# Four-layer cross-attention model: channel chunks summed on the vector engine ahead of the norms' matmuls, and half of a feed-forward projection moved across a loop boundary

## What is computed

```python
x = L0(x, ctx)   # grouped-query cross-attention, + x, then layer norm
x = L1(x, ctx)   # recurrent layer
x = L2(x, ctx)   # norm -> multi-head cross-attention, + x; norm -> 512-2048-512 MLP, + residual
x = L3(x, ctx)   # recurrent layer, same form as L1

# norm, everywhere, over the 512 channels of a token
m = x.mean(-1);  v = ((x - m) ** 2).mean(-1);  y = (x - m) / sqrt(v + eps) * w + b

# recurrent layer
xa = ln(x);  five token-shifted mixes of xa give r, k, v, w, g
s_t = k_t v_t^T + w_t * s_(t-1);  out_t = r_t (u k_t v_t^T + s_(t-1))      # 16x16 state per head
x1 = x + (head_norm(out) * g) @ Wo.T
xc = ln(x1);  sx2 = shift(xc) - xc
xk2 = xc + sx2 * ffn_maa_k;  xr2 = xc + sx2 * ffn_maa_r
return x1 + sigmoid(xr2 @ Wfr.T) * (square(relu(xk2 @ Wfk.T)) @ Wfv.T)
```

## Time and profile before

| | us |
|---|---|
| median of 3 runs | 3214.15 |
| lowest, highest | 3211.52, 3218.05 |
| the profiled execution, its own time | 3217.8 |
| its span in the trace | 3216.0 |
| PE busy | 2880.1 (90%) |
| DVE busy | 1985.7 (62%) |
| ACT busy | 1361.0 (42%) |
| POOL busy | 664.9 (21%) |

### The profile page before, as it was taken

How to read it: one execution, slowest core, us unless ns; L and a number is a source line. 1 busy time by engine, 2 the same in 40 slices (tenths; PEclk the granted TensorE clock), 3 DMA queues, 4 the chain that set the end, 5 groups by cost and what they waited for, 6 DMA issues and landing times.

```text
span 3216.0 us, 54227 instructions
## 1 busy us (share of the span) xinstructions
PE 2880.1 (90%) x18304; PEld 2244.7 (70%) x18304; DVE 1985.7 (62%) x4824; ACT 1361.0 (42%) x3457; POOL 664.9 (21%) x436
## 2 busy tenths in 40 slices
PE   6999998878999999689999998899987889999986
PEld 6555555866888887586545544799987768888866
DVE  2778777348899999523555555210100689999993
ACT  0888887522343333253444444321321233333332
POOL 0011010024444444200000000000000444444440
PEclk9999999978999999799999999899998889999998
DMA  2100100323333333200000000300002333332340
GB/s 102 35 25 31 33 31 3 124 63 93 83 88 88 87 83 93 79 26 19 20 19 27 18 28 1 144 1 0 0 0 85 85 94 86 88 88 83 87 115 19
DMA packets 96305, 182.76 MB, mean 57 GB/s; under 512 B 10138, under 2 KB 87514, under 8 KB 92862
## 3 DMA queue, kind: packets, MB, share of 16 engines
q1 hardware_dynamic: 96190, 181.27, 18.3%
HBM read 171.34 MB, written 9.90 MB: 56 GB/s over the span
## 4 chain that ended last, share of the span: by engine, by line
PE 64%; DVE 13%; issue 11%; ACT 8%; DMA 1%; POOL 1%; DVEq 0%; SPq 0%; ACTq 0%; POOLq 0%
PE psum L466 18%; PE psum L271 11%; PE psum L1812 5%; PE psum L1694 4%; PE psum L1259 3%; DVE psum L665 3%; PE psum L457 2%; ACT arena L1460 2%; ACT arena L2002 2%; PE psum L1749 2%; PE psum L1707 2%; PE psum L473 2%; PE psum L1271 2%; DVE arena L688 2%; PE psum L247 2%
## 5 line engine op out<-in xcount | busy, mean ns | idle before, releaser
L466 PE MATMUL psum<-arena 128*128 128x200 f32 x4096 | 785.9, 351 | 87.1 <-DVE arena L844 34.4
L466 PEld LDWEIGHTS psum<-arena 128*128 128x128 f32 x4096 | 733.6, 200 | 175.5 <-issue 110.2
L1063 POOL TENSOR_TENSOR arena<-arena 128x800 f32<-128x800 f32 x256 | 455.5, 1779 | 513.5 <-DVE psum L665 513.4
L680 DVE TENSOR_TENSOR_SCAN arena<-arena,psum 128x808 f32<-128x808 f32 x256 | 469.9, 1836 | 59.9 <-PE psum L457 47.2
L271 PE MATMUL psum<-arena 128*128 128x200 f32 (+1 forms) x2048 | 354.0, 335 | 21.7 <-DMA arena<-L_w 20.3
L271 PEld LDWEIGHTS psum<-arena 128*128 128x128 f32 x2048 | 351.2, 192 | 23.4 <-DMA arena<-L_w 20.3
L1460 ACT ACTIVATE arena<-arena 100x361 f32<-100x361 f32 x512 | 300.5, 590 | 76.9 <-DVE arena L1371 75.3
L1045 POOL TENSOR_TENSOR arena<-arena 128x800 f32<-128x800 f32 x80 | 140.4, 1755 | 856.0 <-DVE arena L688 695.9
L1371 DVE CUSTOM_DVE_ANT_0 arena<-psum,arena 100x361 f32<-100x361 f32 x512 | 254.0, 529 | 45.5 <-ACT arena L1460 37.9
L665 DVE TENSOR_TENSOR psum<-arena 128x808 f32<-128x808 f32 x256 | 262.5, 1025 | 4.6 <-DVE arena L680 0.5
L1259 PEld LDWEIGHTS psum<-arena 100*128 100x128 f32 x1536 | 145.9, 141 | 131.1 <-ACT arena L1472 60.3
(11 more groups left out here) (129 smaller groups left out, 4069.1 us busy)
## 6 DMA issues: line engine op xcount, KB each, us to landing
arena<-v_rows SPq DMA_DIRECT2D x512, 202.0 KB, 3.2
arena<-ctxT SPq DMA_DIRECT2D x32, 722.0 KB, 4.3
arena<-L_w SPq DMA_DIRECT2D x8, 1152.0 KB, 15.2
arena<-L_w SPq DMA_DIRECT2D x8, 1024.0 KB, 9.8
v_rows<-arena SPq DMA_DIRECT2D x32, 202.0 KB, 2.1
arena<-L_fc SPq DMA_DIRECT2D x4, 1024.0 KB, 7.8
arena<-L_pj SPq DMA_DIRECT2D x4, 1024.0 KB, 15.6
arena<-xT SPq DMA_DIRECT2D x4, 800.0 KB, 9.9
```

What stands on the lines that cost most here:

```text
L466: mm = pe.matmul(chunk(bank, j), m.W[n][:, k, c * P:(c + 1) * P], src[:, k, :], start=k == 0, stop=k == C - 1)
L680: dve.tensor_tensor_scan(m.ring[n % 4].rearrange("p j e -> p (j e)"), m.we[:, cc].rearrange("p j e -> p (j e)"), m.kv, 0.0, ALU.mult, ALU. ...
L1063: pool.tensor_tensor(sv, sv, rb, ALU.mult).then_inc(sem("r_states"), 1)
```

## The change

It has two parts.

**Attention layers' norms.** A class FoldedNorm replaces Norm in L0 and L2 (not in L1 and L3). DVE adds the four channel chunks of a group into one 128x200 tile (tensor_reduce over a view whose innermost axis is the chunk, so consecutive elements read lie 800 bytes apart), and PE then needs one matmul per mean; the squares are treated alike for the variance. The two logarithms of a pair are taken one after the other and then the two exponentials, where before each group had logarithm and exponential together. On PE one group's projection of the next pair now stands between the means and the variances, and the other behind the variances. In L2 ahead of the attention the order becomes: means of t+1, query projection of (t, 0), variances of t+1, query projection of (t, 1).

**Recurrent layers.** fr half 0 moves from the end of a period behind the mean at the start of the next, its tanh moves with it, DVE makes xr2 ahead of step 14 where it stood behind it, and POOL's multiplication of step 13 waits for product 15 where it waited for product 14.

```diff
+class FoldedNorm(Norm):
+    def dve_fold(self, dve, src, i):
+        dve.tensor_reduce(self.fold, src.rearrange("p c n -> p n c"), mybir.AxisListType.X,
+                          ALU.add).then_inc(self.folds.sem, 1)
+    def pe_mean(self, pe, i):
+        pe.wait_ge(self.folds.sem, self.folds.at(i, self.nth))
+        pe.matmul(self.mean_ps, self.core.mean_w, self.fold, start=True, stop=True).then_inc(self.mu.sem, 1)
...
+        pe.matmul(self.var_ps, self.core.mean_w, self.fold, start=True, stop=True).then_inc(self.var.sem, 1)
```

```diff
 # recurrent layers, PE, start of a period
                 m.n1.pe_mean(pe, lambda c: X[:, c, ds(g + 1, N)], f)
+            if tail:
+                wait(pe, "ffn_mix", t, 8)
+                if rec:
+                    wait(pe, "mix_term", i, 20)
...
+                project_half("fr", m.xr2, 0, 4, "ffn_r_sum")
             if back:
                 reduce(6, b)
 # ACT
             if tail:
-                wait(act, "ffn_r_sum", t, 2)
-                act.activation(half(m.thr, 1), full(5), ACT.Tanh, scale=0.5).then_inc(sem("ffn_tanh"), 1)
+                wait(act, "group_done", t)
+                for h in range(2):
+                    wait(act, "ffn_r_sum", t, h + 1)
+                    act.activation(half(m.thr, h), full(4 + h), ACT.Tanh, scale=0.5).then_inc(sem("ffn_tanh"), 1)
 # POOL
                 if rec:
+                    if n == 13:
+                        wait(pool, "kv", i, 16)
                     pool.tensor_tensor(sv, sv, rb, ALU.mult).then_inc(sem("r_states"), 1)
```

```diff
 # L0 behind its attention, PE
             for u in range(2):
-                pe.wait_ge(residual_added.sem, residual_added.at(t, 4 * u + 4))
-                norms[u].pe_mean(pe, lambda c: X[:, c, bass.ds(t * (2 * N) + u * N, N)], t)
+                norms[u].pe_mean(pe, t)
+            if more:
+                pe.wait_ge(residual_added.sem, residual_added.at(t, 4))
+                project(pe, core, 2, Wo, ...)
             for u in range(2):
                 norms[u].pe_var(pe, t)
...
 # DVE
             for u in range(2):
                 dve.wait_ge(residual_added.sem, residual_added.at(t, 4 * u + 4))
+                norms[u].dve_fold(dve, xo(t, u), t)
+            for u in range(2):
                 dve.wait_ge(norm_ready.sem, norm_ready.at(t))
                 norms[u].dve_center(dve, xo(t, u), t)
+            for u in range(2):
+                norms[u].dve_fold_squares(dve, t)
             for u in range(2):
                 norms[u].scale(dve, t)
 # ACT
             for u in range(2):
-                norms[u].act_rstd(act, t)
+                norms[u].act_log(act, t)
+            for u in range(2):
+                norms[u].act_exp(act, t)
```

The order in L2 ahead of the attention, on PE:

```diff
-        statistics(0)
-        statistics(1)
-        queries(0, True)
+        statistics(0)
+        variances(0)
+        for u in range(2):
+            if u == 0:
+                statistics(1)
+            queries(0, u, True)
+            if u == 0:
+                variances(1)
         with pe.Fori(1, pairs - 1) as t:
             statistics(t + 1)
-            queries(t, False)
-        queries(pairs - 1, False)
+            queries(t, 0, False)
+            variances(t + 1)
+            queries(t, 1, False)
+        for u in range(2):
+            queries(pairs - 1, u, False)
```

More of the change, by code:

```diff
@@ L487, in body @@
                 m.n1.pe_mean(pe, lambda c: X[:, c, ds(g + 1, N)], f)
+            if tail:
+                wait(pe, "ffn_mix", t, 8)
+                if rec:
+                    wait(pe, "mix_term", i, 20)
+                elif back:
+                    wait(pe, "bonus", b, 1)
+                project_half("fr", m.xr2, 0, 4, "ffn_r_sum")
             if back:
@@ L839, in body @@
                 mix_term(4)
-            step(14)
             if back:
@@ L845, in body @@
                                              m.xs2[:, c, :, 1:E], ALU.mult, ALU.add).then_inc(sem("ffn_mix"), 1)
+            step(14)
             step(15)
@@ L1031, in body @@
                     act.activation(half(m.kk, h), half(m.ff, h), ACT.Square).then_inc(sem("ffn_squared"), 1)
-                wait(act, "ffn_r_sum", b, 1)
-                wait(act, "group_done", b)
-                act.activation(half(m.thr, 0), full(4), ACT.Tanh, scale=0.5).then_inc(sem("ffn_tanh"), 1)
         turns(act, body)
@@ L1105, in gqa_attention @@
     told = norm_signals(core, name)
-    norms = [Norm(core, told, u, 1, 2 * u, 2 * u + 1).memory(r) for u in range(2)]
+    folds = s("folds", 4)
+    norms = [FoldedNorm(core, told, u, 1, 2 * u, 2 * u + 1).memory(r).signals(folds) for u in range(2)]
     s2 = [n.s2.rearrange("p c n -> p (c n)") for n in norms]
@@ L1563, in mha_attention @@
     told = norm_signals(core, name)
-    norms = [Norm(core, told, u, 0, 2 * u, 2 * u + 1).memory(r) for u in range(2)]
+    folds = s("folds", 4)
+    norms = [FoldedNorm(core, told, u, 0, 2 * u, 2 * u + 1).memory(r).signals(folds) for u in range(2)]
     over = r.at
@@ L1829, in vector @@
         for p in pr:
-            dve.memset(p[:, S:3 * P], 0.0).then_inc(zeroed.sem, 1)
+            dve.memset(p[:, S:3 * P], 0.0)
         def norm_ahead(t):
+            for u in range(2):
+                dve.wait_ge(norms[u].var.sem, norms[u].var.at(t))
+                norms[u].dve_fold(dve, X[:, :, bass.ds(t * (2 * N) + u * N, N)], t)
             for u in range(2):
@@ L1934, in behind_it @@
                 dve.wait_ge(residual_added.sem, residual_added.at(t, 4 * u + 4))
+                norms[u].dve_fold(dve, xo(t, u), t + behind)
+            for u in range(2):
                 dve.wait_ge(fc_sum.sem, fc_sum.at(t))
                 norms[u].dve_center(dve, xo(t, u), t + behind)
+            for u in range(2):
+                norms[u].dve_fold_squares(dve, t + behind)
             for u in range(2):
@@ L2018, in scalar @@
             for u in range(2):
-                norms[u].act_rstd(act, t + behind)
+                norms[u].act_log(act, t + behind)
+            for u in range(2):
+                norms[u].act_exp(act, t + behind)
             for u in range(2):
```

90 lines of the change are left out of this document (55 added, 35 removed).

## The result

The changed kernel takes 3175.6 us (median of 4, 3173.7 to 3181.3), the kernel before beside it 3215.2. The ratio is 0.9878, 95% interval 0.9864 to 0.9891: 39.6 us, or 1.2%, less. The forecast was 3154 in a range of 3138 to 3182. The profiled execution took 3175.7 us with a span of 3173.9, against 3217.8 and 3216.0.

What follows compares the result with a forecast made beforehand. PE, busy 90% of the span, was taken as the bound, with PE and DVE waiting on each other around xr2. -44 (recurrent) and -16 (norms) make -60 from 3217.8: 3157.8, as a median 3154; range 3138 to 3182.

Steps and rivals of the forecast that it cites:

- The wait for xr2 goes, -44 us: Recurrent layers: PE's twelve waits for xr2 and their slow clock, 53.1 us, vanish; net -44 us after charges.
- Slow clock that falls elsewhere, 2 us: Recurrent layers: about 2 us charged against the gain for slow PE clock turning up at other places.
- rival (c): Recurrent layers: only half of 44 caught, DVE and POOL close behind PE, slow clock on 1.14 us waits; 3176, chance 0.15.
- A fold takes 0.98 us: Attention norms: assumed DVE time of one fold of four channel chunks, with 1.84 as the other end.
- 30 us for each microsecond of the fold: Attention norms: some 30 folds in a row, so each microsecond above 0.98 costs 30 us of the total.
- rival (b): Attention norms: folds run at half rate, 1.84 us each, adding 26 us; 3180, chance 0.17.
- 1.6 us of slow clock in a cycle with a gap: Attention norms: PE idle 3.6 us a cycle while DVE folds; 1.6 us charged for 8 cycles, +12.8 us.
- Rival (a): Attention cycles: the clock doesn't fall, as the single mean matmul breaks the gap; -29 instead of -16, 3141, chance 0.13.
- The gain of the norms, -16 us: Attention norms in L0 and L2: net -16 us from fewer matmuls and table loads and new order, after folds and slow clock.
- (d): Attention norms: slower kernel; from folds of 3.0 us the gain is eaten, 3222 at 3.25 us; chance 0.03.
- (e): Recurrent layers: the change doesn't do what it says, something hidden sets the period; 3210, chance 0.02.
- L2 ahead and behind, -21.4 with 8 us of clock on it: L2's norms: -11.2 us ahead of the attention, -10.2 behind it, before the slow-clock charge.

Runs made afterwards that it cites:

- The contiguous fold: Whole change, but the fold of the squares reads four adjacent elements per sum, so other squares are added; fold of X unchanged; 3175.8 us in one run.
- the additions: Whole change, but each fold is made by two DVE additions over adjacent elements in place of the reduction; 3150.2 us, ratio 0.9792.
- the earlier addition: Whole change, but POOL adds the third token mix ahead of its wait for DVE's next product; 3184.3 us, ratio 0.9904.

## Why the prediction was right in sign and short in size

- **The wait for xr2 goes, -44 us.** Right. The recurrent part alone gives 39.6 us by the medians and 22.9 + 20.9 = 43.8 in the two stages of its profiled execution. xr2 took 1.43 us (forecast 1.4), fr half 0 2.87, scan 0 waited 0.24 us (forecast under 0.5), product 0 took 2.48 (forecast about 2.4), and the kernel without POOL's new wait bounds that wait at nothing measurable, inside the 2.4 us set against it.
- **Slow clock that falls elsewhere, 2 us.** Wrong in size, and rival (c) named the place: four periods of each layer have it behind the wait for POOL, 8 x 1.68 = 13.4 us. The trace of before had the sign of it: at 905.20 the low clock was behind POOL's wait, in the one period where it was not behind xr2's. So most periods are 78.4 us or more, and one is the 77.4 of the forecast; the other four intervals of L1 gained 2.6 to 3.4 us each and not 4.3. The sum is right all the same, since the first of the five, which I had at the common 4.3 us, gained 8.5 (89.9 to 81.4). These two errors cancel, and that is luck.
- **A fold takes 0.98 us.** Wrong, and this is the term that was mis-sized. It is 1.51 us. The reason that I gave, a memset over places 404 bytes apart, is a write of few elements and says nothing of a read of 800. The Trainium skill's "Advanced Engine Details and Errata", section SBUF Cachelines, pointed the right way: reads that touch a new 16-byte line each time pay. The contiguous fold bears it out, 985 ns against 1506: half more, not the twice that I had put as the upper end.
- **30 us for each microsecond of the fold.** About right: 0.53 x 30 = 16 us, which eats the -16 of the norms, and by it the sum is 3170, between forecast and rival (b). Measured on the additions the slope is 41; with it the sum is 3154 + 22 = 3176, which is what the kernel takes. That is no second proof, since the slope was taken between this kernel and that one.
- **1.6 us of slow clock in a cycle with a gap.** Right: 1.2, 2.3 and 1.2 us in L0, 1.7, 2.6 and 1.4 in L2 ahead, 1.9 and 1.9 behind, together 14.2 against the 12.8 charged. Filling the gap in L0 brought its three projections back to 5.58 us each. Rival (a), that the clock would hold, is out: the gap has one short matmul in it and the clock falls nonetheless.
- **The gain of the norms, -16 us.** Nothing came (+2.6 us, interval 0 to 5, by itself). Rival (b) names the mechanism and overstates the fold (1.84). Rival (c) gives the same time, 3176, by a cause that is refuted: the recurrent gain was caught in full. Rivals (d) and (e) are out: a fold never came near 3 us, and the period did move.
- **L2 ahead and behind, -21.4 with 8 us of clock on it.** 0.0 as it was built, and with the folds at 0.89 us 1090.6 - 1071.4 = 19.2 us. There the first query projection starts 7.9 us sooner (forecast 8.8), and the way from MLP to MLP is 15.5 us (forecast 15.95). So the chain was right, and the length of its folds was not.

What stays open: what decides behind which wait the low clock falls. Behind the same idle time of 1.13 us it came once before the change and in most periods after it, and behind the 0.70 us ahead of the first projection in L0 it came in one trace (0.87) and not in the other (1.00). The runs show that filling the idle time removes it there, and that it was rarer where the wait was shorter (with the earlier addition it still falls in two of six periods of L1 and in three of L3).

## What to carry to other kernels

Work taken from the engine that bounds the kernel is a gain only where the engine it goes to has time that nobody waits for. The fold of the squares lies behind a projection and brings 16 us; the same fold ahead of the mean has nothing to hide behind and loses 28. Build each half of such a change alone before keeping both, and where a sum over a strided axis is on the path, write it as additions of whole contiguous halves: 0.89 us where the reduction took 1.51.

## What the runs showed of the hardware

A reduction over four elements that stand 800 or 6400 bytes apart took about 1.51 us for 128x800 inputs (the latter 1478 to 1545 ns), over adjacent ones 977 to 987 ns. A matmul of 112 columns in fp32 took 0.23 us, one of 200 columns 0.34 (5.41 us for 16) to 0.38. One matmul in the middle of an idle time of 3.6 us did not keep the clock: the projection behind it was granted 0.69 and took 7.92 us instead of 5.58, and with the idle time filled it was granted 1.00. Behind an idle time of 1.13 us one and the same projection was granted 0.63 in some periods and 1.00 in others. A DVE operation over 128x800 beside a POOL multiplication that had just begun took 2.35 to 2.57 us instead of 0.97 to 1.0, a scan beside one kept its 1.84 us.
